# Projections of a four-layer kernel: the low half of the weights multiplies the high activations alone, in 64-row matmuls on alternating halves of the array

## The reference

```
x = x + layer(_gn(x), ...)                  # _gn: group norm over 32 groups
xn = layernorm(x, norm_w, norm_b)           # over the 64 channels
left  = (xn @ w_left)  * sigmoid(xn @ w_lgate) * mask
right = (xn @ w_right) * sigmoid(xn @ w_rgate) * mask
out = einsum('bikh,bjkh->bijh', left, right)
out = layernorm(out) * sigmoid(xn @ w_ogate)
return out @ w_out
```

## Time and profile before

| | |
|---|---|
| median of 3 runs | 2221.53 us |
| the profiled execution | 2222.49 us, of which the span is 2220.2 us |
| matmuls of line 772 | 8192 (2 x 4096), 8 stages of 1024 |
| mean granted TensorE clock | 0.955 of 2.4 GHz |
| first matmul of a stage to the last, masked (layers 0, 2) | 73.8, 67.8, 72.1, 72.3 us |
| the same, unmasked (layers 1, 3) | 63.7, 67.7, 63.1, 66.0 us |

### The profile page before, as it was taken

The page is one execution under the profiler, slowest core; times in us unless marked ns, Lnnn a source line. Parts: engine busy times, 40 slices in busy tenths (PEclk is TensorE's granted clock), DMA queues, the critical chain, the costliest instruction groups (busy, mean ns, idle before and its releaser), DMA issues. The chain is left out here.

```text
span 2220.2 us, 46598 instructions
## 1 busy us (share of the span) xinstructions
PE 1981.8 (89%) x13950; PEld 1408.4 (63%) x13956; DVE 1736.6 (78%) x2934; ACT 1691.7 (76%) x2730; POOL 625.2 (28%) x590
## 2 busy tenths in 40 slices
PE   5699889779899898989989899899998989899998
PEld 4433868645433887965633497887553359798665
DVE  6588899988688977878958896887775888687665
ACT  3488778779888866859978794776997888595676
POOL 0100647355300000016510190651872000000655
PEclk7799999999999999989999999999999999999999
DMA  9788956379788937358969992926997984663798
GB/s 396 286 253 258 285 139 181 104 259 356 287 253 265 323 106 251 128 209 344 415 226 284 267 233 90 286 80 226 393 404 218 285 302 157 220 221 124 289 347 302
DMA packets 437815, 557.91 MB, mean 251 GB/s; under 512 B 14896, under 2 KB 334384, under 8 KB 421296
## 3 DMA queue, kind: packets, MB, share of 16 engines
q1 hardware_dynamic: 434944, 538.38, 72.6%
q10 hardware_dynamic: 2736, 17.90, 1.9%
HBM read 380.05 MB, written 176.16 MB: 251 GB/s over the span
## 5 line engine op out<-in xcount | busy, mean ns | idle before, releaser
L772 PE MATMUL bank<-whigh,kept 128*128 128x128 f16 x4096 | 507.5, 227 | 59.1 <-DMA kept<-XH 19.0
L772 PEld LDWEIGHTS bank<-whigh,kept 128*128 128x128 f16 x4096 | 466.3, 125 | 68.2 <-issue 57.7
L772 PE MATMUL bank<-wlow,kept 128*128 128x128 f16 x4096 | 506.4, 227 | 1.3 <-issue 1.3
L772 PEld LDWEIGHTS bank<-wlow,kept 128*128 128x128 f16 x4096 | 467.0, 125 | 0.0
L1529 POOL TENSOR_TENSOR LR<-LR 128x512 f32<-128x512 f32 x128 | 187.0, 1480 | 525.0 <-DVE LR L1575 501.2
L794 ACT ACTIVATE sigs<-bank,small 128x256 f32<-128x256 f32 x512 | 236.6, 475 | 62.1 <-PE bank L772 55.6
L1520 POOL TENSOR_TENSOR LR<-LR,sum 128x2048 f32<-128x2048 f32 x30 | 136.6, 4552 | 513.0 <-DVE LR L1338 513.0
L635 PE MATMUL bank<-LR,cen 128*128 128x512 f32 x512 | 256.8, 627 | 21.2 <-DMA LR<-XT 9.2
L691 DVE SCALAR_TENSOR_TENSOR LR<-bank,small,LR 126x1024 f32<-126x1024 f32 x128 | 164.3, 1284 | 120.1 <-ACT LR L668 119.7
L794 ACT ACTIVATE squares<-bank,small 128x256 f32<-128x256 f32 x512 | 236.0, 475 | 13.6 <-PE bank L772 7.2
L643 PE MATMUL bank<-LR,kst 128*128 128x512 f32 x512 | 240.9, 593 | 5.2 <-ACT LR L664 5.2
(11 more groups left out here) (171 smaller groups left out, 3741.0 us busy)
## 6 DMA issues: line engine op xcount, KB each, us to landing
LR<-XT SPq DMA_DIRECT2D x128, 512.0 KB, 5.1
kept<-XH SPq DMA_DIRECT2D x128, 512.0 KB, 5.3
LR<-XT SPq DMA_DIRECT2D x64, 1024.0 KB, 9.6
kept<-XHA SPq DMA_DIRECT2D x128, 512.0 KB, 4.6
XT<-LR SPq DMA_DIRECT2D x48, 1024.0 KB, 8.7
LR<-XH SPq DMA_DIRECT2D x64, 512.0 KB, 6.5
LR<-XHA SPq DMA_DIRECT2D x64, 512.0 KB, 6.1
OS<-kept SPq DMA_DIRECT2D x12, 2048.0 KB, 7.5
```

What stands on the lines that cost most here:

```text
L772: last = pe.matmul(bank(g)[:, j * P:(j + 1) * P], tokens, w[:, half * P:(half + 1) * P], start=part == 0, stop=part == 1)
```

## The change

1. **Low weights meet only the high activations.** The product low x low is left out. A matmul with `wlow` reads the 64 rows of a buffer that hold the high part, instead of all 128.
2. **The rows are laid out by part instead of by channel.** `XH` and `XHA` have the side and the part ahead of the channel. A buffer of side 0 has the high part in rows 0 to 63, and a buffer of side 1 has it in rows 64 to 127. So the 64-row matmuls of side 0 use one half of the array and those of side 1 the other. The constants that lay out the weights follow.
3. **Another order.** The unit of work is two groups, the same four blocks of both sides, in two neighbouring banks. A unit is 8 matmuls with `whigh` over 128 rows, then 8 with `wlow` over 64 rows, sides alternating. All of a unit is signalled at its end.
4. **Without a mask, wider instructions behind it.** ACT and DVE take a unit (512 elements a partition) in one instruction each, instead of two of 256. With a mask they still work by groups.
5. **DMAs.** A chunk is loaded in three DMAs instead of two, with the same bytes. In layers 1 and 3 `norm` stores its result with four DMAs a chunk instead of two, with the same bytes.

```diff
-        XH = nc.dram_tensor("XH", [NT, C, 2, 2, 8, 8, 256], F16).ap()
-        XHA = nc.dram_tensor("XHA", [C, 2, 2, NT, N // 2, P], F16).ap()
+        XH = nc.dram_tensor("XH", [NT, 2, 2, C, 8, 8, 256], F16).ap()
+        XHA = nc.dram_tensor("XHA", [2, 2, C, NT, N // 2, P], F16).ap()
...
-                sp.dma_start(XHA[:, part, :, :, bass.ds(8 * n, 8), :].rearrange("c s t j a -> c s t (j a)"),
-                             xh_cols(buf, k_is_b)).then_inc(stored_.s, 16)
+                for s in range(2):
+                    sp.dma_start(XHA[s, part, :, :, bass.ds(8 * n, 8), :].rearrange("c t j a -> c t (j a)"),
+                                 xh_cols(buf[s::2, :], k_is_b)).then_inc(stored_.s, 16)
...
-            for s in range(2):
-                sp.dma_start(xh_cols(xh_b[h][s], k_is_b), xh_rows(n, s, k_is_b)).then_inc(landed[h].s, 16)
+            sp.dma_start(xh_cols(xh_b[h][0], k_is_b), xh_rows(n, 0, slice(0, 2), k_is_b)).then_inc(landed[h].s, 16)
+            for part in range(2):
+                rows = slice(C * (1 - part), C * (1 - part) + C)
+                sp.dma_start(xh_cols(xh_b[h][1][rows, :], k_is_b), xh_rows(n, 1, slice(part, part + 1), k_is_b)) \
+                    .then_inc(landed[h].s, 16)
...
+                sides_last = [(s, j) for j in range(4) for s in range(2)]
...
-                        for g in range(8):
-                            pe.wait_ge(products_ready.s, products_ready.n + 32 * i + 8 * h + g - 7)
-                            for j in range(4):
...
-                                for part, w in enumerate((whigh, wlow)):
-                                    last = pe.matmul(bank(g)[:, j * P:(j + 1) * P], tokens,
-                                                     w[:, half * P:(half + 1) * P], start=part == 0, stop=part == 1)
-                            last.then_inc(projected.s, 1)
+                        for q in range(4):
+                            unit = 16 * i + 4 * h + q
+                            pe.wait_ge(products_ready.s, products_ready.n + each * unit - 3 * each)
+                            for s, j in sides_last:
+                                pe.matmul(bank(2 * q + s)[:, j * P:(j + 1) * P], tokens(h, s, q, j, slice(0, P)),
+                                          whigh[:, half * P:(half + 1) * P], start=j == 0, stop=False)
+                            for s, j in sides_last:
+                                rows = slice(C * s, C * s + C)
+                                last = pe.matmul(bank(2 * q + s)[:, j * P:(j + 1) * P], tokens(h, s, q, j, rows),
+                                                 wlow[rows, half * P:(half + 1) * P], start=False, stop=j == 3)
+                                if j == 3 and (masked or s == 1):
+                                    last.then_inc(projected.s, 1)
...
+                                act.activation(wide_gate[q], both_sides(q)[:, C:, :, :],
+                                               ACT.Sigmoid, scale=unscale).then_inc(gates_ready.s, 1)
...
+                                dve.scalar_tensor_tensor(dest[:, q // 2, :, :].rearrange("p c (s r) -> p c s r", s=2)
+                                                         [:, :, :, bass.ds(m, 4)],
+                                                         both_sides(q)[:, 0:C, :, :], unscale, wide_gate[q],
+                                                         ALU.mult, ALU.mult).then_inc(products_ready.s, 1)
```

More of the change, by code:

```diff
@@ L595, in norm @@
             cb, k_is_b = small[:, 7:8], layer["k_is_b"]
-            per, tiles = 64 if k_is_b else 32, 2 * NCH
+            per, tiles = 64, 2 * NCH
             kept = P - 2
@@ L723, in project, with both_sides @@
             dest = LRb if layer["low"] else LR
-            gate, unscale = msg if masked else sig, unscales[number % 2]
+            unscale = unscales[number % 2]
             by_vector, by_pool = (1, 5), (0, 2, 3, 4, 6, 7)
+            each = 2 if masked else 1
+            wide_gate = [v[:, u * BANK:(u + 1) * BANK].rearrange("p (c s m) -> p c s m", s=2, m=4)
+                         for v in rings[0] for u in range(2)]
             def where(n, g):
-                if k_is_b:
-                    return g // 4, 16 * n + 4 * (g % 4)
-                return g // 2 % 2, P * (g // 4) + 8 * n + 4 * (g % 2)
+                q, s = divmod(g, 2)
+                return s, 16 * n + 4 * q
+            def both_sides(q):
+                return banks[q][:, :].rearrange("p (s m c) -> p c s m", s=2, m=4)
             @block.sync
@@ L759, in _, with tokens @@
                     pe.wait_ge(sums_taken.s, sums_taken.n)
+                sides_last = [(s, j) for j in range(4) for s in range(2)]
+                def tokens(h, s, q, j, rows):
+                    x = xh_b[h][s]
+                    if k_is_b:
+                        return x.rearrange("p (b r) -> p b r", r=16)[rows, :, 4 * q + j]
+                    return x[rows, (4 * q + j) * P:(4 * q + j + 1) * P]
                 with pe.Fori(0, NCH // 4) as i:
                     for h in range(4):
-                        pe.wait_ge(landed[h].s, landed[h].n + 32 * i + 32)
@@ L779, in _ @@
                     act.preload_act_table_set("sigmoid_and_others")
[L780 to L795 removed]
+                if masked:
+                    with act.Fori(0, NCH // 4) as i:
+                        for h in range(4):
+                            for g in range(8):
+                                group = 32 * i + 8 * h + g
+                                act.wait_ge(projected.s, projected.n + group + 1)
+                                if half == 1 and g >= 4:
+                                    act.wait_ge(summed.s, summed.n)
+                                if g in by_vector:
+                                    act.wait_ge(gate_masked_v.s, gate_masked_v.n + 2 * (4 * i + h) + by_vector.index(g) - 1)
+                                else:
+                                    act.wait_ge(gates_masked.s, gates_masked.n + 6 * (4 * i + h) + by_pool.index(g) - 5)
+                                act.activation(sig[g], bank(g).rearrange("p (m c) -> p c m", m=4)[:, C:, :],
+                                               ACT.Sigmoid, scale=unscale).then_inc(gates_ready.s, 1)
+                else:
+                    with act.Fori(0, NCH // 4) as i:
+                        for h in range(4):
+                            for q in range(4):
+                                unit = 16 * i + 4 * h + q
+                                act.wait_ge(projected.s, projected.n + unit + 1)
+                                if half == 1 and q >= 2:
+                                    act.wait_ge(summed.s, summed.n)
+                                act.wait_ge(products_ready.s, products_ready.n + unit - 3)
+                                act.activation(wide_gate[q], both_sides(q)[:, C:, :, :],
+                                               ACT.Sigmoid, scale=unscale).then_inc(gates_ready.s, 1)
@@ L843, in project @@
+            advance(*((landed[h], 12 * NCH) for h in range(4)), (projected, 4 * each * NCH), (gates_ready, 4 * each * NCH),
+                    (products_ready, 4 * each * NCH))
             if masked:
```

98 lines of the change are left out of this document (42 added, 56 removed).

## The result

| | before | after |
|---|---|---|
| median of 4 runs | 2221.95 us | 3453.36 us |
| lowest to highest | 2219.26 to 2225.62 | 3448.58 to 3462.47 |
| the profiled execution's span | 2220.2 us | 3452.1 us |
| `project`, first to last matmul, layers 0 and 2 | 73.5, 67.5, 71.8, 72.0 us | 84.0, 74.6, 91.9, 82.6 us |
| the same, layers 1 and 3 | 63.4, 67.4, 62.8, 65.7 us | 72.2, 73.9, 81.1, 79.5 us |

The ratio is 1.554, with a 95% interval from 1.5515 to 1.5566. The prediction had the direction right (2235 us, slower) and the size wrong by 1218 us: the time lies far outside the range.

The account below looks back on a forecast made before the run. PE was taken to bound masked and unmasked `project` stages. Matmuls -5.4 and +6.5, instructions behind +4 and DMAs +6.8 made +12 on 2222.5, so 2235 us; range 2183 to 2340 us.

Parts of the forecast that it names:

- Part 3: DMAs: third chunk later at `project` stage starts through extra stores and a third load DMA, +6.8 us; elsewhere nothing.
- Part 1: Steady-state `project` matmuls: pairs overlap fully, changes of rows cost 0.09 us plus a load; -5.4 us unmasked, +6.5 masked.
- A: Rival: changes of rows cost nothing between short 16-bit matmuls in `project`; 2196 us, chance 0.25.
- B: Rival: the two halves do not run beside each other at all in `project`; 2343 us, chance 0.17.
- D: Rival: each change of half empties the array as a change of rows does; near 2670 us, chance 0.03.
- C: Rival: halves overlap where tokens lie side by side, but masked loads go one after another; 2293 us, chance 0.11.
- Part 2: ACT and DVE behind `project` matmuls: no steady-state gain, each stage end +0.5 us, +4 us over eight stages.
- The clock: A granted clock falling within a stage, as half the array is used, would upset the forecast; set at nothing.

Follow-up runs that it names:

- e1: The kernel before, with only the `finish` loads of `XH` and `XHA` walked side first instead of channel first: 3333.16 us.
- e11: The kernel before, with side 1's chunk loaded by two 256 KB DMAs cut by tokens, each into all 128 rows: 2225.65 us, ratio 1.002.
- e4: The kernel before, with side 1's chunk loaded by two DMAs, into rows 0 to 63 and 64 to 127: 2306.69 us, ratio 1.0366.
- e5: The changed kernel, with side 1's parts swapped in DRAM so its chunk is one 128-row DMA, and `finish` loads channel first into 128 rows: 2247.42 us.
- e10: As e5, but masked layers work by groups with 128-row matmuls, and unmasked units alternate high-low and low-high: 2206.94 us, ratio 0.9932.
- e7: As e5, but low matmuls use all 128 rows again (low x low is back), in the same runs of eight: 2246.16 us.
- e9: As e5, but all low matmuls, side 1's too, read rows 0 to 63: 2708.75 us, ratio 1.2195.

## Why the prediction was right and wrong

**Failed: Part 3, "The loads of `finish` move the same bytes in as many DMAs: nothing."** I counted bytes and DMAs and not how a DMA walks. Side first, the same 512 KB run at 53 GB/s instead of some 300 to 440: +1111 us by e1, nine tenths of the result. So the direction came out right mostly by luck: 1206 of the 1231 us come from loads that Part 3 had at nothing. No rival was near it, since all four were about the array.

**Failed: Part 3, "In the steady state SP issues three DMAs in some 2 us for each 3.5 us chunk, hidden by the three chunks loaded ahead."** The issue is hidden, as e11 shows (+4 us). The transfer isn't: two of the three go into 64 rows, and 85 us came of it in e4: 39 in the masked stages, whose engines were already full at 268 GB/s, and 43 in the unmasked ones, which had a share of 0.86. Both shares stood in my own first reading; any change to these loads had to be priced there.

**Right: Part 1.** Forecast 0.872 us an unmasked unit, measured 0.883 (e5); 1.036 masked, measured 1.046. Full overlap of a pair held. A change of rows at 0.09 held, read off float32 rows of another stage, and so did a load of its own of 0.01 or 0.05. On these four numbers rivals A, B and D fall: there is a gap at each change, low matmuls come in pairs, and a change of half costs nothing; C falls by the masked unit. The two of a pair start 0.003 us apart; the 4 ns of the Trainium skill (TensorE: Matmul & The Clock Gate, Part 3), which no row of before could show, agree with it. (The estimate that the prediction made of them is half of what it should be: two pairs a group at 4 ns are 0.008 us a group, over 448 groups +3.6 us and not +1.8. The sum doesn't use it.)

**Right in kind, off in size: the start of the stages.** PE's wait for kept chunks at six stage starts grew by 11 us in all in e5 (3.5, 6.4, 4.0, 5.2, 1.4 and 6.9 us before; 3.9, 7.1, 7.3, 8.6, 4.1 and 7.4 in e5). Not all of this is time lost, since other waits there became shorter: the first four chunks of the eight stages took 183.4 us instead of 178.5, +4.9. The first stages of layers 1 and 3, where the extra stores stand ahead of the third chunk, took +6.0 together, the other six -1.1. Part 3 had 2 x 1.27 = 2.5 us for these stores; its third DMA doesn't exist in e5. Part 2's stage end came out at 1.84 instead of 1.36 us unmasked, so +0.5 as forecast, but masked at 2.80 instead of 2.96, so nothing.

**The sum for e5.** Without the third DMA the forecast is -5.4 + 6.5 + 4 + 2.5 = +8 us. The span grew by 25. That e5 lies only 12 us above 2235 is in part luck: the 2235 hold 4 us for a third DMA that e5 lacks, and start 1 us higher than the kernel before of e5's batch. The eight stages grew by 12.7 (556.9 - 544.2): +4.9 in the first four chunks, and in the other twelve -2.3 unmasked and +10.1 masked, where Part 1 had -5.4 and +6.5. Of the +10.1, 4.0 lie in the stage whose chunks were all loaded at its start (layer 0, half 1), where PE waits for DVE. A further 12 us stand outside the stages, where the forecast had 4.

The masked loss comes with the unit of two groups: with groups as before it is gone (-0.5 over whole masked stages in e10), with units on all rows it is there (+8.9 in e7, +10.0 in e5). The part outside the stages is in all three (12, 10 and 11 us), so it is due neither to rows nor to masked units. What all three share are the layout in DRAM by part, the stores side by side, the wide instructions and the gate's doubled constants; I haven't separated these.

**The clock** was 1.00 in the `project` windows of e5, with both halves in use, so setting it at nothing was right there. In `finish` it fell with PE's waits: 0.70 from 512 to 540 us of the changed kernel, and 0.68 in e1, which has none of the new matmuls. e9 shows that the worry was not idle: with one half alone it stayed at 0.50.

## What to carry to other kernels

Before a layout is changed, follow every DMA that reads it, and compare not bytes and counts but the outermost dimension that each side walks and the number of rows it writes: 2 outermost entries cost a factor of six to eight here, and 64 rows instead of 128 in a half of the loads made the `project` stages 15% longer (544 to 626 us in e4). Where the DMA engines are full or nearly so, that is the first place to price. Matmuls of 64 rows on two halves run two at a time, but this pays only if the changes of rows are rare: at eight a run it is nearly even, and reversing the order in every other unit halves the changes without taking more banks.

## What the runs showed of the hardware

- The rate of a DMA followed its outermost dimension: 53 GB/s at a DMA share of 0.13 with 2, 105 at two tenths with 4, 26 for each.
- Two DMAs of 256 KB into 64 rows each, instead of 128, held an unmasked stage at 239 GB/s with a share of 1.07, against 278 with a share of 0.84. In the changed kernel a masked stage had 189 GB/s at 1.12.
- 64-row matmuls on two halves ran in pairs at 0.056 us a pair, weight loads included, and also where the program has four of one half and then four of the other (0.027 us each on average).
- A change between 128 and 64 rows cost 0.09 to 0.10 us each way for float16, near the 0.08 to 0.10 of float32, and lengthened the next interval by 0.01 us, or by 0.05 where the tokens lie 16 elements apart.
- With one half alone 64-row matmuls were 0.056 us apart at the full clock, as 128-row ones (1.10 us a unit). After the wait for the third chunk the granted clock stayed at 0.50 (1.2 GHz) to the end of the stage, with PE never idle; with both halves it was back at 1.00 after some 4 us.
